# Shared expert: last group up and last two groups down as three single-pass products, with the parts formed in the tail

## The chip, the cores and the metric

The kernel runs on 1 core of one Trainium2 chip. The time is the device time of one execution in microseconds (us). The span of a profile runs from the first to the last instruction; the execution's own time is a little longer. Engines: TensorE (PE, its weight loads PEld), VectorE (DVE), ScalarE (ACT), GpSimd (POOL) and SyncE (SP), which issues most DMAs.

## The reference

Inputs: x of 64 x 32 x 512 in float32, that is 2048 tokens of 512, and a condition vector of 128 for each of the 64 blocks. In essence:

```python
h   = gelu(gelu(cond @ W0 + b0) @ W1 + b1); att = softmax(h @ W2 + b2)
xt  = einsum(att-weighted 32x32 matrices, x) + att @ bias_k    # 2048 tokens x 512
scores = softmax(xt @ router_w + router_b) + router_bias       # 16 experts, 4 groups of 4
# keep the best 2 groups, then the best 2 experts: gate, idx
y   = sum over the 2 chosen experts of gate * ((silu(xt@w1+b1) * (xt@w2+b2)) @ w3 + b3)   # inner width 128
z   = (silu(xt @ sw1 + sb1) * (xt @ sw2 + sb2)) @ sw3 + sb3    # the shared expert, inner width 256, all tokens
out = x + y + z
```

Everything is float32. This case concerns z, the shared expert.

## The kernel before, in words

The 2048 tokens are 16 tiles of 128; 4 tiles make a group (`GT` = 4, `NG` = 4 groups, 0 to 3; `EARLY` = 2, `LAST` = 3). `C` = 4 slices of 128 of the model width, `IB` = 2 blocks of 128 of the shared inner width. The order on each engine is the order written out by hand in that engine's block; engines wait for one another by counting semaphores.

**Stages.** First the mixing, the transposed activations `xT[:, g, c, :]`, the router, and the shared expert for groups 0 and 1 (upward, L891 on ACT, `shared_up` on PE; downward `shared_down`). Then a loop over tiles of tokens sorted by expert: gather by POOL, up, hidden, down on PE, scatter by POOL. Then the tail, which is what the change touches.

**Two forms of a product.** `shared_up(g, i)` (L644) sums, for w = 0, 1 and c = 0 to 3, a product of a 128x128 weight with 512 tokens. For groups 0 and 1 both operands had been split into a high part and a rest of type float32r (ACT copies the high part, L863; POOL subtracts to get the rest, L476), and the product is made of three matmuls (`PRODUCTS`: high*high, high*rest, rest*high). For groups 2 and 3 it is one float32 matmul of `sw12` and `xT`. A float32 matmul stands in the profile as two MATMUL records, a float32r one as one. `shared_down(g)` (L667) makes, for each of 4 tiles, two float32 matmuls of the hidden values `gs_of(g)` with `sw3_sb`, and one bf16 matmul with gates and biases (L687).

**The tail before the change.** PE (L806 to L815): `shared_up(2, 0)` with the last expert tile's last two steps between, `shared_up(2, 1)`, `shared_up(3, 0)`, `shared_up(3, 1)`, `shared_down(2)`, `shared_down(3)`. Blocks are numbered n = 2g + i; `shared_up` waits for `up_ready` at n - 1 (L650), which frees its PSUM bank. In `shared_down`, tile t from 8 on waits for `z_ready` at t - 3 (L679), so tile 12 waits for DVE's addition of tile 8. ACT (L968 to L977): the last expert result (L933), `shared_silu(2)`, `shared_silu(3)` (L886), then, when the rows of group 3 are loaded, four scalings (L977). POOL: the last scatter, then four additions of the scaled rows (L552), each after one scaling. DVE (L1284 to L1291): `shared_hidden(2)` (L1115, bias and multiply, two instructions), `add_rows(0)`, `add_rows(1)`, `shared_hidden(3)`, `add_rows(2)`, `shared_sum(2)`, `add_rows(3)`, `shared_sum(3)`. `add_rows(g)` (L1276) is 8 multiply-adds of expert rows into the sums (4 for group 3) and waits for the rows of its group; `shared_sum(g)` (L1196, seen as L990) adds the four PSUM tiles. SP: after the last scatter it issues 8 loads of expert rows, 2 for each group in order (L394), then stores of the 16 result tiles, each when its sum is ready (L349).

The large array `wexp` (expert weights) is free once the last expert tile is done; the rows, the hidden values of group 2 (`gs_third`) and, with the change, new parts lie in it.

Of the kernel before, what the change touches and what calls it, by code (L numbers as in the profile page):

```python
# [5 lines left out]
P = 128  # L6
ALU = mybir.AluOpType
# [12 lines left out]
def adaln_moe_ffn(nc, x, cond_pack, router_pack, shared_pack, expert_pack, expert_bias, down_bias, out):  # L20
# [40 lines left out]
    with ctx:  # L61
# [16 lines left out]

        wexp = sb("wexp", [P, E, EW])
        ebias = sb("ebias", [P, E, 2, INTER])  # L80
        shared_sb = sb("shared_sb", [P, 2 * C * SHARED + IB * DIM])
        sw12 = shared_sb[:, 0:2 * C * SHARED].rearrange("p (w c n) -> p w c n", w=2, c=C)
        sw3_sb = shared_sb[:, 2 * C * SHARED:].rearrange("p (i n) -> p i n", i=IB)

        x_early = sb("x_early", [P, EARLY * GT, DIM])
        late_region = sb("late_region", [P, 16384 // 4])
        xT = sb("xT", [P, NG, C, GN])
        r1 = sb("r1", [P, 8192 // 4])
        xt_sb = sb("xt_sb", [P, 8192 // 4])
# [35 lines left out]
        def early(rows, cols):  # L125
# [41 lines left out]
                   + [spare[:, u * DIM:(u + 1) * DIM] for u in range(2)])  # L167
        gs_third = wexp_flat[:, NG * TOPK * GT * DIM:NG * TOPK * GT * DIM + IB * GN].rearrange(
            "p (i n) -> p i n", i=IB)

# [111 lines left out]
        x_again_loaded = sem("x_again_loaded")  # L282
        rows_loaded = [sem(f"rows_loaded{g}") for g in range(NG)]
        last_scaled = sem("last_scaled")
        last_added = sem("last_added")
# [24 lines left out]
        def split_of(n):  # L310

            u = (n + EARLY * GT) % SPLITS if n < SPLITS - EARLY * GT else n - (SPLITS - EARLY * GT)
            if u < EARLY * GT:
                g, cols = u // GT, slice((u % GT) * P, (u % GT + 1) * P)
                return xT[:, g, :, cols], x_split[:, g, 0, :, cols], x_split[:, g, 1, :, cols]
            n = 2 * C * SHARED // 4
            cols = slice((u - EARLY * GT) * n, (u - EARLY * GT + 1) * n)
            return shared_sb[:, cols], w_split[:, 0, cols], w_split[:, 1, cols]

        def load_mixed(engine, g, row_groups):  # L320
# [81 lines left out]
        def _(pool):  # L402
# [143 lines left out]
            scatter(to_slot[:, :], 1)  # L546

            pool.wait_ge(x_again_loaded, 16 * (NT - EARLY * GT))
            for u in range(GT):
# [7 lines left out]
        def _(pe):  # L557
# [86 lines left out]
            def shared_up(g, i, between=()):  # L644
# [6 lines left out]
                for w in range(2):  # L651
                    for c in range(C):
                        cols = slice(i * P, (i + 1) * P)
                        if g < EARLY:
                            for n_product, (a, b) in enumerate(PRODUCTS):
                                last = mm(psum[:, bank + w, :], w12_split[:, a, w, c, cols], x_split[:, g, b, c, :],
                                          start=(c == 0 and n_product == 0),
# [9 lines left out]
            def shared_down(g, tiles=range(GT)):  # L667
                pe.wait_ge(up_ready, IB * (g + 1))
                for t in (g * GT + u for u in tiles):
# [8 lines left out]
                    elif t >= 8:  # L678
                        pe.wait_ge(z_ready, t - GT + 1)  # L679
                    bank = psum[:, DOWN_BANKS[t], :]  # L680
                    for i in range(IB):
                        mm(bank, gs_of(g)[:, i, (t % GT) * P:(t % GT + 1) * P], sw3_sb[:, i, :],
                           start=(i == 0), stop=False)

# [113 lines left out]
            with pe.If(pairs > SURE + 2):  # L798
                with pe.Fori(1, (PAIRS - SURE) // 2) as j:
                    for q in range(2):  # L800
                        p = j * 2 + SURE + q
                        with pe.If(pairs > p):
# [6 lines left out]
                                     (0, 2): lambda: down(1, last_expert, tiles, tiles_less_2)})  # L809
            shared_up(2, 1)  # L810
            shared_up(3, 0)
            shared_up(3, 1)
            pe.wait_ge(y_ready, tiles)
            shared_down(2)
            shared_down(3)  # L815


        @block.scalar
        def _(act):
# [149 lines left out]
            result(1, 1, tiles, count_of(act, N_SCATTERED + 2))  # L969
            shared_silu(2)  # L970
            shared_silu(3)

# [8 lines left out]
        def _(dve):  # L981
# [301 lines left out]

            shared_hidden(2)  # L1284
            add_rows(0)
            add_rows(1)
            shared_hidden(3)
            add_rows(2)
# [60 lines left out]
```

## Time and profile before

| what | value |
|---|---|
| median of 3 runs | 258.35 us (254.38, 258.35, 259.02) |
| the profiled execution | 256.43 us, span 254.7 us, so 1.7 us lie outside the span |
| busy share of the span | PE 92%, DVE 52%, POOL 44%, ACT 32% |
| expert loop | about 91 us to 205 us |
| tail | 205 us to 254.7 us |
| last instruction that computes | DVE's addition of tile 15, at 251.54 us |

Times in the rows are microseconds from the span's start, durations marked ns are nanoseconds. "x16" is the number of instructions; the brackets say how long the engine had been idle and what released it.

### The profile page before, as it was taken

The page shows a single profiled execution, that of the slowest core. Times are in us where ns is not written, and L with a number is a line of the kernel's source. Part 1 is how long each engine was busy: PE and PEld are TensorE (multiplying, and loading weights), DVE is VectorE, ACT ScalarE, POOL GpSimd, SP SyncE. Part 2 cuts the span into 40 slices and gives each one's busy share as a digit, 9 for nine tenths or more (in the row PEclk, how much of TensorE's full clock was granted, in tenths as well). Part 3 has the DMA queues.
Part 4 walks back from the last instruction along what each step waited for, and adds up shares of the span by engine and source line. Part 5 has one row for each costly group of instructions (what it writes and reads, how often), then busy time and mean ns, then how long its engine had stood idle before and what let it go on. Part 6 is the DMA issues. An engine that isn't in the chain of part 4 may idle for free.

```text
span 254.7 us, 3970 instructions
## 1 busy us (share of the span) xinstructions
PE 233.7 (92%) x1126; PEld 152.7 (60%) x1127; DVE 131.8 (52%) x266; ACT 81.5 (32%) x177; POOL 111.3 (44%) x136
## 2 busy tenths in 40 slices
PE   4959897999998899999999999999999699999695
PEld 4936544788744467677777777777777244444241
DVE  1294952199998873333333333333333101598982
ACT  1322787231490003333333333333333111111400
POOL 6177455900203554666656666666643310000720
PEclk9985999799999999999999999999999889999979
DMA  7999999999098389545544454555542205999753
GB/s 195 273 289 321 415 414 419 410 423 367 40 373 368 86 249 364 171 165 165 165 153 144 152 159 133 165 165 165 165 165 84 90 0 221 393 388 387 300 200 129
DMA packets 21930, 60.03 MB, mean 236 GB/s; under 512 B 2613, under 2 KB 2741, under 8 KB 21660
## 3 DMA queue, kind: packets, MB, share of 16 engines
q1 hardware_dynamic: 15164, 39.93, 42.3%
q0 software_dynamic: 5600, 17.83, 21.7%
q10 hardware_dynamic: 1152, 2.10, 2.9%
q8 instruction: 7, 0.11, 0.2%
q14 instruction: 7, 0.06, 0.1%
HBM read 43.07 MB, written 17.30 MB: 237 GB/s over the span
## 4 chain that ended last, share of the span: by engine, by line
PE 67%; DVE 20%; DMA 5%; issue 4%; ACT 2%; DVEq 0%; ACTq 0%
PE psum L559 57%; DVE late_region L990 6%; PE psum L735 6%; DMA xt_rows<-r 3%; PE psum L605 3%; DVE xT L1276 3%; DMA xT<-cond_pack 2%; DVE xT L990 2%; PE psum L748 2%; DVE r L990 1%; DVE x_early L990 1%; DVE mixed_w L1027 1%; ACT r L839 1%; DVE r L1232 0%; ACT x_split L863 0%
## 5 line engine op out<-in xcount | busy, mean ns | idle before, releaser
L559 PE MATMUL psum<-wexp,r 128*128 x272 | 68.7, 382 | 0.5 <-DVE r L1232 0.3
L559 PEld LDWEIGHTS psum<-wexp,r 128*128 128x128 f32 x272 | 48.3, 190 | 23.7 <-issue 17.7
L990 DVE TENSOR_TENSOR r<-psum,ebias 128x256 f32<-128x256 f32 x34 | 14.4, 424 | 65.2 <-PE psum L559 65.2
L508 POOL DMA_INDIRECT expert_rows<-late_region,to_row x33 | 33.4, 1011 | 33.3 <-ACT late_region L933 30.3
L498 POOL DMA_INDIRECT late_region<-xt_rows,from_row x36 | 35.3, 980 | 17.9 <-issue 8.8
L559 PE MATMUL psum<-wexp,xt_sb 128*128 x68 | 34.8, 594 | 0.0
L559 PE MATMUL psum<-xT,shared_sb 128*128 128x512 f32 x64 | 29.7, 621 | 2.5 <-issue 2.5
L927 ACT ACTIVATE r<-r 128x128 f32<-128x128 f32 x34 | 10.5, 309 | 55.6 <-DVE r L990 55.6
L933 ACT ACTIVATE late_region<-psum 128x512 f32<-128x512 f32 x34 | 20.3, 597 | 16.1 <-PE psum L559 16.1
L1232 DVE COPY r<-psum 128x512 f32<-128x512 f32 x36 | 24.5, 680 | 0.0
L559 PE MATMUL psum<-x_split,w_split 128*128 128x512 f32 x96 | 23.8, 409 | 0.3 <-DVE logits L990 0.3
L559 PEld LDWEIGHTS psum<-xT,shared_sb 128*128 128x128 f32 x64 | 12.5, 199 | 18.5 <-issue 18.5
L735 PE MATMUL psum<-ident,late_region 128*128 128x128 f32 x144 | 21.6, 273 | 0.9 <-DMA late_region<-xt_rows,from_row 0.9
L559 PEld LDWEIGHTS psum<-x_split,w_split 128*128 128x128 f32 x96 | 18.9, 199 | 4.5 <-DVE logits L990 0.4
L735 PEld LDWEIGHTS psum<-ident,late_region 128*128 128x128 f32 x144 | 17.9, 141 | 5.4 <-issue 1.9
L923 ACT ACTIVATE xt_sb<-psum 128x128 f32<-128x128 f32 x34 | 9.4, 278 | 19.7 <-PE psum L748 19.7
L552 POOL TENSOR_TENSOR xt_sb<-xt_sb,wexp 128x512 f32<-128x512 f32 x2 | 3.5, 1748 | 27.1 <-ACT wexp L977 27.1
L476 POOL TENSOR_TENSOR x_split<-xT,x_split 128x512 fp32r<-128x512 f32 x8 | 10.0, 1275 | 4.0 <-ACT x_split L863 4.0
L1041 DVE COPY xT<-psum 128x512 f32<-128x512 f32 x12 | 8.2, 687 | 6.7 <-PE psum L605 6.5
L559 PE MATMUL psum<-ident 128*128 128x128 f32 x52 | 10.0, 359 | 1.6 <-POOL ident L411 1.6
L1115 DVE SCALAR_TENSOR_TENSOR wexp<-psum,router_sb,wexp 128x512 f32<-128x512 f32 x2 | 1.5, 750 | 19.1 <-ACT wexp L886 19.1
L559 PE MATMUL psum<-shared_sb,late_region 128*128 128x512 f32 x16 | 9.1, 700 | 2.1 <-DVE xT L990 2.1
(191 smaller groups left out, 291.3 us busy)
## 6 DMA issues: line engine op xcount, KB each, us to landing
wexp<-expert_pack SPq DMA_DIRECT2D x16, 768.0 KB, 9.4
wexp<-expert_rows SPq DMA_DIRECT2D x8, 1024.0 KB, 12.9
xt_rows<-xt_sb SPq DMA_DIRECT2D x8, 256.0 KB, 8.5
xt_rows<-r SPq DMA_DIRECT2D x8, 256.0 KB, 8.8
x_early<-x SPq DMA_DIRECT2D x1, 2048.0 KB, 15.2
ebias<-expert_bias SPq DMA_DIRECT2D x1, 2048.0 KB, 11.4
out_dram<-x_early SPq DMA_DIRECT2D x8, 256.0 KB, 9.7
shared_sb<-shared_pack SPq DMA_DIRECT2D x1, 1536.0 KB, 19.6
```

The lines of the kernel that those rows point to most:

```text
L476: T.tensor_tensor(rest, whole, part, ALU.subtract).then_inc(split_ready, 1)
L498: nc.gpsimd.indirect_dma_start(out=xg[:, i % RING, :], out_offset=None, in_=xt_dram[:, :], in_offset=bass.IndirectOffsetOnAxis(ap=from_row ...
L508: nc.gpsimd.indirect_dma_start(out=y_dram[:, :], out_offset=bass.IndirectOffsetOnAxis(ap=rows.bitcast(U32), axis=0), in_=y_sb[:, slot, :], ...
L559: return nc.tensor.matmul(dst, lhsT, rhs, start=start, stop=stop)
L605: last = nc.tensor.transpose(psum[:, bank_of(t), c * P:(c + 1) * P], xt_ring[t % XR][:, c * P:(c + 1) * P], ident[:, :])
L735: last = nc.tensor.transpose(psum[:, b, c * P:(c + 1) * P], xg[:, slot, c * P:(c + 1) * P], ident[:, :])
L923: nc.scalar.activation(gT_sb[:, b, :], psum[:, 4 + b, 0:P], ACT.Copy).then_inc(gT_ready, 1)
L927: nc.scalar.activation(s_sb[:, b, :], h_sb[:, b, 0, :], ACT.Silu).then_inc(s_ready, 1)
L933: nc.scalar.activation(y_sb[:, slot, :], psum[:, 6 + b, :], ACT.Copy).then_inc(y_ready, 1)
L990: return nc.vector.tensor_tensor(dst, a, b, op)
L1041: V.tensor_copy(xT[:, t // GT, :, (t % GT) * P:(t % GT + 1) * P], psum[:, bank_of(t), :].rearrange("p (c n) -> p c n", c=C)).then_inc(xT_r ...
L1232: V.tensor_copy(xgT[:, b], psum[:, b, :].rearrange("p (c n) -> p c n", c=C)).then_inc(xgT_ready, 1)
```

## The change

Group 3's upward products and the downward products of groups 2 and 3 take the three-matmul form. Their parts are formed in the tail, beside what was there:

- ACT, after the last expert result: 8 copies for the high parts of `sw12` (4) and `xT[:, 3]` (4), then SiLU of block (2, 0), 2 copies for `sw3`, the copy of hidden block (2, 0), SiLU (2, 1), copy (2, 1), and then for each block of group 3 its SiLU and its copy, the copy waiting for DVE's hidden value.
- DVE: 8 subtractions for the rests of `sw12` and `xT[:, 3]`; `shared_hidden(2, [1])` is now behind `add_rows(0)`; after `shared_hidden(LAST)` come 2 subtractions for the rests of group 3's hidden values.
- POOL: 2 subtractions for `sw3` and 2 for the hidden values of group 2, between the last scatter and the additions of rows.
- PE: a wait for the 8 parts ahead of `shared_up(3, 0)`, waits for the parts ahead of each `shared_down`.
- Rests are written over the wholes or into `r1`; high parts go to the free end of `wexp`. No DMA is added.

```diff
...
@@ -165,8 +171,22 @@
                    + [spare[:, u * DIM:(u + 1) * DIM] for u in range(2)])
-        gs_third = wexp_flat[:, NG * TOPK * GT * DIM:NG * TOPK * GT * DIM + IB * GN].rearrange(
-            "p (i n) -> p i n", i=IB)
+        gs_at = NG * TOPK * GT * DIM
+        gs_third = wexp_flat[:, gs_at:gs_at + IB * GN].rearrange("p (i n) -> p i n", i=IB)
+        free_part = wexp_part[:, :, :].rearrange("p e n -> p (e n)")[:, gs_at + IB * GN:]
+        n12, n3, ngs = 2 * C * SHARED, IB * DIM, IB * GN
+        w12_last = [a.rearrange("p (w c n) -> p w c n", w=2, c=C) for a in (free_part[:, 0:n12], r1_part[:, :])]
+        w3_late = [a.rearrange("p (i n) -> p i n", i=IB)
+                   for a in (free_part[:, n12:n12 + n3], shared_part[:, n12:])]
+        x_last = [free_part[:, n12 + n3:n12 + n3 + C * GN].rearrange("p (c n) -> p c n", c=C),
+                  xT_part[:, NG - 1, :, :]]
+        gs_parts = {g: [a.rearrange("p (i n) -> p i n", i=IB) for a in (free_part[:, at:at + ngs], low)]
+                    for g, at, low in (
+                        (2, n12 + n3 + C * GN,
+                         wexp_part[:, :, :].rearrange("p e n -> p (e n)")[:, gs_at:gs_at + ngs]),
+                        (3, n12 + n3 + C * GN + ngs, late_part[:, 0:ngs]))}
         ident = sb("ident", [P, P])
...
@@ -316,6 +343,16 @@
             return shared_sb[:, cols], w_split[:, 0, cols], w_split[:, 1, cols]
+        LAST_SPLITS = 2 * C
+        def last_split_of(n):
+            c = n % C
+            if n < C:
+                w, c0 = n // 2, 2 * (n % 2)
+                return [a[:, w, c0:c0 + 2, :] for a in (sw12, *w12_last)]
+            return [a[:, c, :] for a in (xT[:, NG - 1], *x_last)]
         def load_mixed(engine, g, row_groups):
...
@@ -545,6 +582,15 @@
             scatter(to_slot[:, :], 1)
+            for i in range(IB):
+                pool.wait_ge(w3_hi_ready, i + 1)
+                T.tensor_tensor(w3_late[1][:, i], sw3_sb[:, i], w3_late[0][:, i], ALU.subtract
+                                ).then_inc(w3_lo_ready, 1)
+            for i in range(IB):
+                pool.wait_ge(gs_hi_ready, i + 1)
+                T.tensor_tensor(gs_parts[2][1][:, i], gs_of(2)[:, i], gs_parts[2][0][:, i], ALU.subtract
+                                ).then_inc(gs_lo_ready, 1)
             pool.wait_ge(x_again_loaded, 16 * (NT - EARLY * GT))
...
@@ -651,9 +697,11 @@
                         cols = slice(i * P, (i + 1) * P)
-                        if g < EARLY:
+                        if g != 2:
                             for n_product, (a, b) in enumerate(PRODUCTS):
-                                last = mm(psum[:, bank + w, :], w12_split[:, a, w, c, cols], x_split[:, g, b, c, :],
+                                weights = w12_split[:, a, w, c, cols] if g < EARLY else w12_last[a][:, w, c, cols]
+                                x_cols = x_split[:, g, b, c, :] if g < EARLY else x_last[b][:, c, :]
+                                last = mm(psum[:, bank + w, :], weights, x_cols,
                                           start=(c == 0 and n_product == 0),
...
@@ -678,9 +726,14 @@
                     bank = psum[:, DOWN_BANKS[t], :]
+                    cols = slice((t % GT) * P, (t % GT + 1) * P)
                     for i in range(IB):
-                        mm(bank, gs_of(g)[:, i, (t % GT) * P:(t % GT + 1) * P], sw3_sb[:, i, :],
-                           start=(i == 0), stop=False)
+                        if g < EARLY:
+                            mm(bank, gs_of(g)[:, i, cols], sw3_sb[:, i, :], start=(i == 0), stop=False)
+                        else:
+                            for n_product, (a, b) in enumerate(PRODUCTS):
+                                mm(bank, gs_parts[g][b][:, i, cols], w3_late[a][:, i, :],
+                                   start=(i == 0 and n_product == 0), stop=False)
                     if t == 0:
...
@@ -808,10 +861,14 @@
             shared_up(2, 1)
+            pe.wait_ge(last_lo_ready, LAST_SPLITS)
             shared_up(3, 0)
             pe.wait_ge(y_ready, tiles)
+            pe.wait_ge(w3_lo_ready, IB)
+            pe.wait_ge(gs_lo_ready, IB)
             shared_down(2)
+            pe.wait_ge(gs_last_lo_ready, IB)
             shared_down(3)
...
@@ -967,8 +1024,23 @@
             result(1, 1, tiles, count_of(act, N_SCATTERED + 2))
-            shared_silu(2)
-            shared_silu(3)
+            for m in range(LAST_SPLITS):
+                whole, hi, _ = last_split_of(m)
+                nc.scalar.activation(hi, whole, ACT.Copy).then_inc(last_hi_ready, 1)
+            def hidden_hi(g, i):
+                act.wait_ge(up_ready, g * IB + i + 1)
+                nc.scalar.activation(gs_parts[g][0][:, i], gs_of(g)[:, i], ACT.Copy).then_inc(gs_hi_ready, 1)
+            shared_silu(2, [0])
+            for i in range(IB):
+                nc.scalar.activation(w3_late[0][:, i], sw3_sb[:, i], ACT.Copy).then_inc(w3_hi_ready, 1)
+            hidden_hi(2, 0)
+            shared_silu(2, [1])
+            hidden_hi(2, 1)
+            for i in range(IB):
+                shared_silu(3, [i])
+                hidden_hi(3, i)
             act.wait_ge(rows_loaded[LAST], 16 * TOPK)
...
@@ -1281,10 +1353,23 @@
                         link(ins)
-            shared_hidden(2)
+            for m in range(LAST_SPLITS):
+                dve.wait_ge(last_hi_ready, m + 1)
+                whole, hi, lo = last_split_of(m)
+                tt(lo, whole, hi, ALU.subtract).then_inc(last_lo_ready, 1)
+            def hidden_lo(i):
+                dve.wait_ge(gs_hi_ready, IB + i + 1)
+                tt(gs_parts[LAST][1][:, i], gs_of(LAST)[:, i], gs_parts[LAST][0][:, i], ALU.subtract
+                   ).then_inc(gs_last_lo_ready, 1)
+            shared_hidden(2, [0])
             add_rows(0)
+            shared_hidden(2, [1])
             add_rows(1)
-            shared_hidden(3)
+            shared_hidden(LAST)
+            for i in range(IB):
+                hidden_lo(i)
             add_rows(2)
...
```

## Rows read from the trace of the kernel before

**Rows 1.** The page: busy shares; the chain that ended last, by engine.

```profile
PE 233.7 (92%) x1126; PEld 152.7 (60%) x1127; DVE 131.8 (52%) x266; ACT 81.5 (32%) x177; POOL 111.3 (44%) x136
...
PE 67%; DVE 20%; DMA 5%; issue 4%; ACT 2%; DVEq 0%; ACTq 0%
```

**Rows 2.** Chain of waits, 205 to 255 us: start, us, what.

```profile
205.12 26.90 PE psum L559 x62
...
241.00 0.70 DVE xT L990
...
241.84 9.69 PE psum L559 x20
...
251.54 0.69 DVE xT L990
```

**Rows 3.** Timeline of DVE: start, us, line, tiles [idle before].

```profile
219.76 11.08 DVE L1276 SCALAR_TENSOR_TENSOR x_early<-wexp,tops,x_early 128x512 f32<-128x512 f32 x16
...
233.43 7.54 DVE L1276 SCALAR_TENSOR_TENSOR xT<-wexp,tops,xT 128x512 f32<-128x512 f32 x8
241.00 2.48 DVE L990 TENSOR_TENSOR xT<-xT,psum 128x512 f32<-128x512 f32 x4
```

**Rows 4.** Timeline of ACT from 204 us.

```profile
207.15 0.60 ACT L933 ACTIVATE late_region<-psum 128x512 f32<-128x512 f32 x1 [1.72 <-PE psum L559]
211.44 0.69 ACT L886 ACTIVATE wexp<-psum,router_sb 128x512 f32<-128x512 f32 x1 [3.70 <-PE psum L559]
218.31 0.69 ACT L886 ACTIVATE wexp<-psum,router_sb 128x512 f32<-128x512 f32 x1 [6.18 <-PE psum L559]
...
232.04 0.69 ACT L886 ACTIVATE late_region<-psum,router_sb 128x512 f32<-128x512 f32 x1 [6.18 <-PE psum L559]
```

**Rows 5.** Timeline of PEld, 45 to 70 us: weight loads of block (1, 0), three products.

```profile
63.48 5.33 PEld L559 LDWEIGHTS psum<-x_split,w_split 128*128 128x128 f32 x24
```

**Rows 6.** Timeline of PE, two tiles of the downward product of group 2.

```profile
231.84 1.88 PE L559 MATMUL psum<-shared_sb,wexp 128*128 128x512 f32 x4
...
233.78 1.88 PE L559 MATMUL psum<-shared_sb,wexp 128*128 128x512 f32 x4
```

**Rows 7.** Timeline of ACT, 44 to 71 us: four copies of high parts.

```profile
43.90 2.18 ACT L863 ACTIVATE x_split<-xT 128x512 fp32r<-128x512 f32 x4
```

**Rows 8.** Instructions of lines 863 and 476: ns min/median/max, first and last start.

```profile
L863 ACT ACTIVATE x_split<-xT x8: 617/626/657, 34.7 to 45.5; 128x512 fp32r<-128x512 f32 x8
...
L476 POOL TENSOR_TENSOR x_split<-xT,x_split x8: 1271/1274/1278, 35.6 to 48.3; 128x512 fp32r<-128x512 f32 x8
```

**Rows 9.** Line 394 alone at 212.2 us: the second load of rows.

```profile
L394 SPq DMA_DIRECT2D wexp<-expert_rows x1: 495/495/495, 212.2 to 212.2; - x1
DMA to landing us min/median/max: 7.5/7.5/7.5
```

**Rows 10.** Timeline of ACT: the scalings, released by the last load.

```profile
236.10 2.56 ACT L977 ACTIVATE wexp<-wexp,tops 128x512 f32<-128x512 f32 x4 [3.37 <-DMA wexp<-expert_rows]
```

**Rows 11.** Timelines of DVE and POOL, 236 to 242 us, where both run.

```profile
236.19 1.42 DVE L1276 SCALAR_TENSOR_TENSOR xT<-wexp,tops,xT 128x512 f32<-128x512 f32 x2
237.52 1.77 DVE L1276 SCALAR_TENSOR_TENSOR xT<-wexp,tops,xT 128x512 f32<-128x512 f32 x1
239.22 1.75 DVE L1276 SCALAR_TENSOR_TENSOR xT<-wexp,tops,xT 128x512 f32<-128x512 f32 x1
236.97 3.45 POOL L552 TENSOR_TENSOR xt_sb<-xt_sb,wexp 128x512 f32<-128x512 f32 x2 [27.08 <-ACT wexp L977]
240.38 2.95 POOL L552 TENSOR_TENSOR xT<-xT,wexp 128x512 f32<-128x512 f32 x2
```

**Rows 12.** Busy time by stretch, PE alone: stretch, busy (count), PEclk.

```profile
240.00:241.00 1.00, 0.00 (x0) 1.00 0.29 111
...
243.00:244.00 1.00, 1.00 (x2) 0.54 1.01 375
...
246.00:247.00 1.00, 1.00 (x3) 0.75 0.00 0
```

More of the change, by code:

```diff
@@ L76, in adaln_moe_ffn, with sb_and_parts @@
         HALF = E // 2
-        wexp = sb("wexp", [P, E, EW])
+        def sb_and_parts(name, shape):
+            with nc.sbuf_tensor(name + "_part", shape, F32R) as part:
+                pass
+            return sb(name, shape), part
+        wexp, wexp_part = sb_and_parts("wexp", [P, E, EW])
         ebias = sb("ebias", [P, E, 2, INTER])
-        shared_sb = sb("shared_sb", [P, 2 * C * SHARED + IB * DIM])
+        shared_sb, shared_part = sb_and_parts("shared_sb", [P, 2 * C * SHARED + IB * DIM])
         sw12 = shared_sb[:, 0:2 * C * SHARED].rearrange("p (w c n) -> p w c n", w=2, c=C)
@@ L85, in adaln_moe_ffn @@
         x_early = sb("x_early", [P, EARLY * GT, DIM])
-        late_region = sb("late_region", [P, 16384 // 4])
-        xT = sb("xT", [P, NG, C, GN])
-        r1 = sb("r1", [P, 8192 // 4])
+        late_region, late_part = sb_and_parts("late_region", [P, 16384 // 4])
+        xT, xT_part = sb_and_parts("xT", [P, NG, C, GN])
+        r1, r1_part = sb_and_parts("r1", [P, 8192 // 4])
         xt_sb = sb("xt_sb", [P, 8192 // 4])
@@ L283, in adaln_moe_ffn @@
         rows_loaded = [sem(f"rows_loaded{g}") for g in range(NG)]
+        last_hi_ready = sem("last_hi_ready")
+        last_lo_ready = sem("last_lo_ready")
+        w3_hi_ready = sem("w3_hi_ready")
+        w3_lo_ready = sem("w3_lo_ready")
+        gs_hi_ready = sem("gs_hi_ready")
+        gs_lo_ready = sem("gs_lo_ready")
+        gs_last_lo_ready = sem("gs_last_lo_ready")
         last_scaled = sem("last_scaled")
```

## The prediction

> **What bounds the kernel now.** I read the page first, then the chain of waits of the tail, then each engine's timeline over the same stretch. PE is busy 92% of the span, and the chain of work is PE's for 67% of it [rows 1]. That share is an average over stages, though. The change touches only what comes after 205 us, so the chain there is what counts [rows 2]. It is PE's own for 26.9 us, to 232.0 us. Then it leaves PE: it runs through DVE's additions of expert rows to 241.0 us. PE has group 2 down done at 239.6 us (four tiles from 231.84 us, each 1.94 us after the one before [rows 6]) and then waits for DVE's first sum at 241.0 us. The last four tiles are PE's again, 241.84 to 251.52 us, and DVE's last addition starts at 251.54 us.
>
> So a faster PE before 241 us is worth nothing by itself; what DVE does from 219.76 us on sets when the last four tiles may begin. DVE's list is full there: 16 multiply-adds in 11.08 us (0.693 us each), group 3's hidden values, and `add_rows(2)` in 7.54 us from 233.43 us [rows 3]. It is this list that the change makes longer and ties to ACT.
>
> **The change part by part.** All times are on the profiled execution, 256.43 us with a span of 254.7 us; the median of the runs is 258.35 us, 1.9 us more.
>
> *PE, shorter products.* A float32 block of `shared_up` takes 6.87 us (the SiLUs that end them stand at 211.44 and 218.31 us) [rows 4]. The same block in three passes: 24 weight loads in 5.33 us, so (5.33 - 0.19) / 23 = 0.2235 us each and 5.36 us a block [rows 5]. Saved: 1.5 us a block, 3.0 us for two. A downward tile goes from 1.94 us (231.84 to 233.78) [rows 6] to 6 + 1 instructions of 0.2235 = 1.56 us; saved 0.38 us a tile, 1.5 us a group. In all 6.0 us of PE work go.
>
> *Parts of the weights and of xT.* ACT ends the last expert result at 207.75 us [rows 4]. Eight copies at 0.545 us (four took 2.18) [rows 7] end at 212.1 us. DVE's eight subtractions: no row has this subtraction on DVE; the first can begin 0.63 us [rows 8] after 207.75 us. Below stands 0.62 us each (four additions with one operand in PSUM in 2.48 us), above 1.75 us (two SBUF operands while POOL also runs) [rows 3, 11]; POOL is nearly idle there, so I take 0.65 us, 208.4 to 213.6 us; by the upper end it is 222.4 us. PE needs them at 218.3 us, so they cost nothing in the forecast; the cover is `shared_up(2)`, and by the upper end PE would wait 4 us. SiLU (2, 0) moves from 211.44 to 212.1 us and its hidden value to 213.6 us, also covered. ACT's two copies of `sw3` end at 213.9 us; POOL's subtractions at 1.27 us [rows 8] end near 217.3 us with the first hidden block, against a need at 231 us: nothing.
>
> *`shared_hidden(2, [1])` behind `add_rows(0)`.* This is the first new wait. `add_rows(0)` waits for the rows of group 0, that is the second load: 212.2 + 7.5 = 219.7 us [rows 9]. Its 8 instructions (5.54 us) end at 225.2 us, the hidden value of (2, 1) at 225.95 us instead of 219.8 us. Block (3, 1) is n = 7 and waits for `up_ready` at 6, which is this value. PE, after 218.3 + 5.36 = 223.6 us, stands still until 226.0 us: 2.4 us, most of the 3.0 us just saved. Behind the same value on ACT stand its copy (2, 1) and then SiLU (3, 0), so these move to 226 to 227.2 us.
>
> *POOL against `add_rows(1)`.* POOL's subtraction for (2, 1) runs at about 226.6 us, while DVE is in `add_rows(1)`. What such a meeting costs is in [rows 11]: a multiply-add takes 1.75 to 1.77 us beside POOL against 0.7 us alone (two in 1.42 us), so 1.0 us. `add_rows(1)`: 225.95 + 5.54 + 1.0 = 232.5 us (bounds 0 and 1.0).
>
> *The ladder for group 3.* This is the second new wait, and the dearer one. Before, both SiLUs of group 3 were done or ready when DVE came, and DVE went on at 233.43 us. Now ACT may not do SiLU (3, 1) before its copy of block (3, 0), and that copy waits for DVE. In order: DVE hidden (3, 0) 232.5 to 233.2; ACT copy 0.63, to 233.8, then SiLU (3, 1), 0.69, to 234.5 [rows 4, 8]; DVE hidden (3, 1) to 235.3; ACT copy to 235.9; DVE's two subtractions, one behind hidden (3, 1) and one behind the copy, to 236.6. PE's block (3, 1) is done by 226.0 + 5.36 = 231.4 us, before its SiLU is asked for, so PE's gain buys nothing here. `add_rows(2)` starts at 236.6 us instead of 233.43 us: 3.1 us late.
>
> *`add_rows(2)` against POOL.* The last load lands at 236.0 us and frees the scalings at 236.10 us [rows 10]; ACT is free at 235.9 us. So POOL's four additions start at 237.0 us as before. Before, half of `add_rows(2)` was over by then and two of its instructions were slowed, by 1.0 us each [rows 11]. Now all of it lies beside POOL. Bounds: two slowed as before, or four, one for each of POOL's additions. I take three, since in [rows 11] the second of the pair from 236.19 us kept its length (it ended at 237.61 us) although POOL had begun at 236.97 us. That is 5.54 + 3.0 = 8.6 us, ending at 245.2 us (244.2 to 246.2), 4.2 us later than before.
>
> The Trainium skill, GPSIMD Engine Reference, in its table of specifications, says that POOL's SBUF interfaces are shared with VectorE and contend with DVE instructions in a 2-port mode or with two SBUF inputs. Taken to the letter every overlapped multiply-add pays, which makes it four and 1.0 us more at the end; the first instruction in the rows did not pay.
>
> *The last four tiles.* The first sum frees tile 12 at 245.2 + 0.84 = 246.0 us (before, 241.00 to 241.84). PE has had nothing since 231.4 + 4 x 1.56 = 237.6 us, 8.4 us. Before, it paused 2.2 us, and the granted clock was then about 0.5 from 243 us to the middle of the microsecond that shows 0.75, so some 3.4 us [rows 12], 1.2 GHz instead of 2.4, a loss of about 1.7 us. Four tiles warm are 6.2 us. With one such stretch: 6.2 + 1.7 + 0.2 = 8.1 us, PE done at 254.1 us; with two, 255.8 us. Before it took 9.68 us. So of group 3's 1.5 us all stays, and DVE's chain has eaten it first. I take one stretch and half of another's risk: last addition at 254.8 us against 251.54 us. The last store behind it is unchanged.
>
> **Sum.** +3.1 (ladder, first wait and POOL) + 1.0 (POOL in `add_rows(2)`) + 0.1 - 1.6 (last tiles) + 0.7 (clock) = +3.3 us. On the profiled execution 259.7 us; on the median 261.6 us. The runs before spread over 4.6 us, and the profiled one lies 1.9 us under the median; I put 260.5 us, between the two.
>
> **The rivals.**
> *A, PE's gain comes through (faster side, within 2%).* If DVE's waits turned out free (`add_rows(2)` at 233.4 us, ending 241.0 us), only the last tiles would shrink: 241.84 + 8.1 = 249.9 us, 1.6 us less: 254.8 us profiled, 256.7 us on the median. For it: 6.0 us of PE work really go, and PE holds 67% of the chain. Against it: `shared_hidden(2, [1])` stands in the code behind a load that lands at 219.7 us.
> *B, the clock (slower by over 2%).* The place is the last four tiles and block (3, 1). If PE stays at the low level for all 28 products of the last four tiles, they take 28 x 0.447 = 12.5 us instead of 8.1, so the last addition starts at 258.5 us: +7.0 us, 263.4 us profiled, 265.4 us on the median. It decides from +5.2 us, that is from 1.9 us more loss than I count, 3.8 us more at the low level. For it: PE now pauses twice, 2.4 us and 8.4 us, where 2.2 us were followed by half the clock. Against: after that pause it was back within 5 us of work.
> *C, a wash.* The three overlaps with POOL do not bite and the ladder is cheaper than its steps (copies 0.55 us): the delay of 4.2 us shrinks to 1.6 us, which the tiles give back; 258.4 us on the median. That is also what would be seen if the three-pass blocks did not run in 5.36 us but as slowly as before and DVE alone decided.
>
> **How the numbers follow.** Forecast 0.60, A 0.13, B 0.15, C 0.12. The range 256.5 to 264.5 us holds A's time, C, and the forecast with its bounds (two or four slowed instructions, one or two slow stretches: -1.7 to +2.7 us); B's far part is left out. A difference of 2%, 5.2 us, is about what a measurement of this kernel can tell from no change. Faster by over 2% would need more than the 1.6 us that any chain here offers: 0.03. Slower by over 2%: B and the upper end of the forecast, 0.18. Within 2%: 0.79.
>
> **What would show it.** In the changed profile: 24 weight loads of a block of group 3 in about 5.3 us; PE idle about 2.4 us before block (3, 1), released by DVE's hidden value near 226 us; DVE idle in front of the second hidden value of group 3, released by ACT; `add_rows(2)` starting near 236.6 us with three multiply-adds above 1.5 us; PE idle some 8 us before tile 12 and a granted clock near 0.5 after it. I am wrong if `add_rows(2)` starts before 235 us, or if PE goes from (3, 0) to (3, 1) without a pause, or if the subtractions on DVE take over 1 us each.

## The result: 1.9% slower, and where it went

The changed kernel takes 259.83 us in the median (257.5 to 262.4, 4 runs) against 256.47 us (254.38 to 259.02, 4 runs) of the kernel before: ratio 1.0192, 95% interval 1.0128 to 1.0257. The ratio compares only the faster executions of each kernel, so it is not the quotient of the two medians, which is 1.013. Run again beside other kernels later it gave 1.0191 (1.0119 to 1.0264). The profiled execution took 258.33 us with a span of 256.5 us.

The profiles differ by only 1.9 us. Their stages ahead of the tail, which the change does not touch, differ too: the last expert result ends at 207.75 us before and at 206.03 us after. More of the early work ran at half clock in the profile of before; that this is all of the 1.7 us is not shown. Busy time of each engine in one early stretch, with PEclk (the granted clock of PE as a share of 2.4 GHz) third from the end, before and after:

```profile
40.00:50.00 10.00, 8.16 (x42) 5.93 (x42) 1.41 (x5) 4.58 (x9) 7.75 (x7) 0.83 1.04 417
```

```profile
40.00:50.00 10.00, 8.17 (x46) 6.04 (x46) 1.52 (x5) 4.29 (x8) 8.00 (x7) 1.00 1.03 416
```

I measure everything from the end of the last expert result: the **tail**, to the end of DVE's last addition, is 44.48 us before (252.23 - 207.75) and 47.99 us after (254.02 - 206.03). That is +3.5 us, 1.4% of the time; the ratio's interval begins at 1.3%. In a second profile of the changed kernel (below) the tail is 49.33 us, +4.85 us or 1.9%.

The page after (busy; the chain by engine), for [rows 1]:

```profile
PE 226.1 (88%) x1158; PEld 157.1 (61%) x1159; DVE 140.8 (55%) x276; ACT 89.0 (35%) x191; POOL 116.6 (45%) x140
...
PE 53%; DVE 24%; DMA 13%; issue 5%; ACT 3%; SPq 0%; DVEq 0%; POOL 0%; POOLq 0%; ACTq 0%
```

PE has lost 7.6 us of busy time and the kernel is slower: PE's share of the chain fell from 67% to 53%, DVE's and DMA's grew. The chain of waits of the tail (start, us, what), for [rows 2]:

```profile
210.48 7.55 DMA wexp<-expert_rows
218.03 0.03 issue
218.06 2.75 DVE x_early L1348 x4
...
223.57 0.66 DVE wexp L1187
...
230.67 0.67 DVE late_region L1187
231.34 0.02 issue
231.37 0.63 ACT wexp_part L1033
232.00 0.59 ACT late_region L943
232.58 0.03 issue
232.61 0.76 DVE late_region L1187
233.37 0.02 issue
233.39 0.64 ACT wexp_part L1033
...
244.97 8.34 PE psum L605 x28
253.31 0.02 issue
253.33 0.69 DVE xT L1062
```

Before, PE stood in this chain until 232.0 us. Now, from 210.48 us on, the chain is the load of group 0's rows and then DVE, and between 230.67 and 233.39 us it climbs the ladder: DVE hidden block, ACT copy, ACT SiLU, DVE hidden block, ACT copy. DVE's timeline, for [rows 3]:

```profile
224.15 6.52 DVE L1348 SCALAR_TENSOR_TENSOR x_early<-wexp,tops,x_early 128x512 f32<-128x512 f32 x8
230.59 0.74 DVE L1187 SCALAR_TENSOR_TENSOR late_region<-psum,router_sb,late_region 128x512 f32<-128x512 f32 x1
232.61 0.75 DVE L1187 SCALAR_TENSOR_TENSOR late_region<-psum,router_sb,late_region 128x512 f32<-128x512 f32 x1 [1.28 <-ACT late_region L943]
233.28 1.47 DVE L1062 TENSOR_TENSOR late_region_part<-late_region,wexp_part 128x512 fp32r<-128x512 f32 x2
234.67 9.43 DVE L1348 SCALAR_TENSOR_TENSOR xT<-wexp,tops,xT 128x512 f32<-128x512 f32 x8
```

POOL's four additions stand beside the last of these lines:

```profile
235.44 3.46 POOL L598 TENSOR_TENSOR xt_sb<-xt_sb,wexp 128x512 f32<-128x512 f32 x2 [8.75 <-ACT wexp L1049]
238.86 3.37 POOL L598 TENSOR_TENSOR xT<-xT,wexp 128x512 f32<-128x512 f32 x2
```

`add_rows(2)` starts 28.64 us into the tail instead of 25.68, and takes 9.4 us instead of 7.5. PE's waits from 220 us on (engine, line, what for: us in total, times, longest), and its granted clock (stretch, busy, PEclk), for [rows 12]:

```profile
PE psum L605 <- DVE xT L1062: 6.9, 1, 6.9
PE psum L605 <- DVE wexp L1187: 2.3, 1, 2.3
```

```profile
224.00:228.00 4.00, 3.71 (x9) 0.57 1.05 387
241.00:245.00 4.00, 0.03 (x1) 0.58 0.00 0
245.00:246.00 1.00, 1.00 (x3) 0.50 0.41 127
...
248.00:249.00 1.00, 1.00 (x5) 0.77 0.34 123
```

Both pauses are there and in this profile both are followed by work at 1.2 GHz. The account: +2.96 (later start of `add_rows(2)`), +1.90 (its length, to the first sum), -1.35 (from the first sum to the end, 11.23 to 9.88 us) = +3.5 us.

### The profile page after: what moved, and what is told of

It is laid out like the page before. It is cut to its first block, busy times and chain, and to the rows that moved or that the text cites. A ratio compares the mean times of both kernels' runs of the same rounds, so it can differ in the third digit from the quotient of the medians.

```text
span 256.5 us, 4064 instructions
## 1 busy us (share of the span) xinstructions
PE 226.1 (88%) x1158; PEld 157.1 (61%) x1159; DVE 140.8 (55%) x276; ACT 89.0 (35%) x191; POOL 116.6 (45%) x140
## 4 chain that ended last, share of the span: by engine, by line
PE 53%; DVE 24%; DMA 13%; issue 5%; ACT 3%; SPq 0%; DVEq 0%; POOL 0%; POOLq 0%; ACTq 0%
PE psum L605 45%; DVE late_region L1062 6%; PE psum L788 6%; DVE x_early L1348 4%; DMA xt_rows<-xt_sb 4%; DMA xt_rows<-r 3%; DVE xT L1348 3%; DMA wexp<-expert_rows 3%; DMA xT<-cond_pack 2%; PE psum L801 2%; PE psum L651 1%; DVE r L1062 1%; DMA expert_rows<-late_region,to_slot 1%; DVE xT L1062 1%; DVE x_early L1062 1%
## 5 line engine op out<-in xcount | busy, mean ns | idle before, releaser
L605 PE MATMUL psum<-wexp_part 128*128 128x512 f32 x40 | 17.5, 470 | 9.2 <-DVE xT L1062 6.9
L605 PE MATMUL psum<-x_split,w_split 128*128 128x512 f32 x96 | 22.4, 392 | 0.6 <-DVE logits L1062 0.3
L605 PEld LDWEIGHTS psum<-x_split,w_split 128*128 128x128 f32 x96 | 17.9, 188 | 4.6 <-DVE xt_sb L1187 0.5
L605 PE MATMUL psum<-xT,shared_sb 128*128 128x512 f32 x32 | 14.2, 595 | 2.8 <-issue 2.8
L605 PEld LDWEIGHTS psum<-wexp_part 128*128 128x128 f32 x40 | 8.4, 211 | 11.6 <-issue 7.4
L1348 DVE SCALAR_TENSOR_TENSOR x_early<-wexp,tops,x_early 128x512 f32<-128x512 f32 x16 | 12.0, 810 | 6.0 <-DMA wexp<-expert_rows 5.9
L605 PEld LDWEIGHTS psum<-xT,shared_sb 128*128 128x128 f32 x32 | 5.9, 190 | 10.6 <-issue 10.6
L1348 DVE SCALAR_TENSOR_TENSOR xT<-wexp,tops,xT 128x512 f32<-128x512 f32 x10 | 10.8, 1136 | 0.0
```

The lines of the kernel that those rows point to most:

```text
L605: return nc.tensor.matmul(dst, lhsT, rhs, start=start, stop=stop)
L1348: ins = V.scalar_tensor_tensor(out=acc_tile(t), in0=rows_k[:, g, k, t % GT, :], scalar=tops[:, k, t:t + 1], in1=acc_tile(t), op0=ALU.mult, ...
```

## Experiments

All tails are from the end of the last expert result to the end of DVE's last addition. "Start" is that of `add_rows(2)`, "length" from there to the first sum of group 2, "rest" what follows. Each row's times are those of one profiled execution. Each ratio is against the kernel before on the same chip. The intervals are 0.7 to 2% wide, so what 1 or 2 us between two kernels come from is read from the traces, not from the ratios.

| kernel | start | length | rest | tail | ratio (95%) |
|---|---|---|---|---|---|
| before | 25.68 | 7.57 | 11.23 | 44.48 | 1 |
| changed | 28.64 | 9.47 | 9.88 | 47.99 | 1.019 (1.013-1.026) |
| changed, again | 28.85 | 9.47 | 11.01 | 49.33 | 1.019 (1.012-1.026) |
| e1_order | 28.33 | 9.45 | 9.64 | 47.42 | 1.024 (1.018-1.030) |
| e2_order_silu | 26.87 | 9.45 | 10.40 | 46.72 | 1.011 (1.003-1.019) |
| e3_down3_f32 | 27.12 | 9.50 | 12.30 | 48.92 | 1.022 (1.012-1.032) |
| e10_down3_order | 25.47 | 7.55 | 12.38 | 45.40 | 1.012 (1.006-1.018) |
| e4_warm | 28.54 | 9.47 | 8.23 | 46.24 | 1.019 (1.009-1.029) |
| e9_before_warm | 25.68 | 7.57 | 9.54 | 42.79 | 0.999 (0.992-1.005) |
| e6_after_no_pool | 28.58 | 5.54 | 10.41 | 44.53 | 1.007 (1.003-1.012) |
| e7_before_no_pool | 25.68 | 5.54 | 10.41 | 41.63 | 0.989 (0.982-0.996) |
| e5_up_only | 24.96 | 5.54 | 9.63 | 40.13 | 0.982 (0.976-0.988) |
| e8_up_no_pool | 24.50 | 5.54 | 10.41 | 40.45 | 0.984 (0.980-0.987) |

**The changed kernel again** (no edit).

> The changed kernel once more, unedited, beside the two kernels of this call. Tail 47.5 to 48.5 us; add_rows(2) starts 28.3 to 28.9 us after the last expert result and takes 9.4 to 9.5 us; time 1.3 to 2.5% above the kernel before. If instead the tail is near 46 us, the first profile of it was not typical and the account of 3.5 us falls.

Start and length repeat to 0.2 us. The tail is 0.8 us above the expected band, all in the last tiles, 9.46 us instead of 8.34. PEclk of this run:

```profile
244.00:246.00 2.00, 1.58 (x4) 0.50 0.42 156
...
248.00:250.00 2.00, 2.00 (x6) 0.50 0.07 26
250.00:252.00 2.00, 2.00 (x10) 0.91 0.36 134
```

Half clock lasted 6.0 us into the last tiles here, past 250 us, against 3.5 us in the first profile. The length of such a stretch after a long pause varies from run to run; the delay of DVE does not.

PE's first pause went the other way. It was 2.5 us long, and block (3, 1) behind it ran at full clock, 5.7 us from 223.72 us on, where it took 7.4 us at first. PE's wait, and then its PEclk:

```profile
PE psum L605 <- DVE wexp L1187: 2.5, 1, 2.5
```

```profile
223.00:229.00 6.00, 5.28 (x23) 1.00 1.05 387
```

The start of `add_rows(2)` moved by only 0.2 us, so the half clock of that block did no harm in this kernel.

**Order, step one** (e1_order).

```diff
-            shared_hidden(2, [0])
+            shared_hidden(2)
             add_rows(0)
-            shared_hidden(2, [1])
             add_rows(1)
```

> The changed kernel with group 2's second hidden block ahead of add_rows(0) again, as it was before the change. Measure: the tail, from the end of the last expert result on ACT to the end of DVE's last addition, 44.5 us before the change (207.75 to 252.23) and 48.0 us after it (206.03 to 254.02). Theory (DVE's list and its ladder with ACT decide): PE's pause of 2.3 us ahead of block (3, 1) goes, so PE is done with that block 2 to 4 us sooner, but the ladder still begins when add_rows(1) ends, so add_rows(2) starts at most 0.7 us sooner and the tail stays at 47.3 to 48.0 us. Rival (PE's pause is what costs): the tail falls by 2.3 us or more, to 45.7 us or below.

47.42 us, as the theory said. PE's first pause is gone, and its block (3, 1) ends early for nothing: ACT's copy of block (3, 0) waits 8.3 us for DVE.

```profile
234.05 0.74 DVE L1187 SCALAR_TENSOR_TENSOR late_region<-psum,router_sb,late_region 128x512 f32<-128x512 f32 x1
236.07 0.75 DVE L1187 SCALAR_TENSOR_TENSOR late_region<-psum,router_sb,late_region 128x512 f32<-128x512 f32 x1 [1.27 <-ACT late_region L943]
...
234.83 0.63 ACT L1033 ACTIVATE wexp_part<-late_region 128x512 fp32r<-128x512 f32 x1 [8.30 <-DVE late_region L1187]
```

**Order, step two** (e2_order_silu), e1's edit and:

```diff
+            shared_silu(3)
             for i in range(IB):
-                shared_silu(3, [i])
                 hidden_hi(3, i)
```

> As the kernel with group 2's second hidden block ahead of add_rows(0), and on ACT both SiLUs of group 3 ahead of both copies; the work is the same as after the change. Theory: the rungs of the ladder go. DVE does both hidden blocks back to back (1.4 us), one copy stays in the open (0.63 us), then two subtractions (1.3 us). Against the order SiLU, copy, SiLU, copy that saves DVE's wait of 1.28 us and a part of the copy, so add_rows(2) starts about 1.0 to 1.3 us sooner; with POOL's four additions at the same time as before, one of them meets less, so the tail is 46.0 to 47.2 us. Rival (the work of the subtractions, not the order, costs; or the end is set by PE): 47.5 us or more.

46.72 us, within the band. The start falls by 1.5 us against e1, though not one copy or subtraction was removed: that is the price of the rungs. The length did not fall; even at 26.87 us all four of the second half's multiply-adds are still ahead when POOL begins.

**Group 3's downward product in float32** (e3_down3_f32; the rest of `sw3` also goes to its own place, so that the whole stays).

```diff
-                        if g < EARLY:
+                        if g != 2:
                             mm(bank, gs_of(g)[:, i, cols], sw3_sb[:, i, :], start=(i == 0), stop=False)
...
-                shared_silu(3, [i])
-                hidden_hi(3, i)
+            shared_silu(3)
...
-            for i in range(IB):
-                hidden_lo(i)
```

> The changed kernel with group 3's downward product as float32 again: no copies and no subtractions of its hidden blocks, everything else as after the change. Theory: add_rows(2) starts after add_rows(1) and two hidden blocks, 2.6 us sooner than in the changed kernel, so that fewer of its multiply-adds meet POOL (two or three instead of four, 1 to 2 us); the last four tiles take 1.5 us more at full clock, 9.7 us or so. Tail 44.5 to 46.0 us. Rival (PE's last tiles decide): the tail grows by 1.5 us, to 49.5 us.

A miss: the tail stayed at 48.92 us. The start fell by only 1.5 us instead of 2.6, and no meeting with POOL was saved. The chain of waits says what took the ladder's place:

```profile
227.62 0.67 DVE wexp L1185
...
228.34 7.35 PE psum L606 x24
...
235.72 0.70 ACT late_region L943
```

DVE's late hidden value (2, 1) lets PE's block (3, 1) begin, and that block, 3.4 us of it at half clock after the pause, takes 7.35 us. Its PEclk (stretch, busy, PEclk):

```profile
228.00:230.00 2.00, 1.66 (x5) 0.78 1.05 387
230.00:232.00 2.00, 2.00 (x6) 0.50 1.04 384
232.00:234.00 2.00, 2.00 (x9) 0.87 1.05 387
```

So PE's first pause, harmless behind the ladder, was the next bound, together with the half clock after it. That was not in my theory, and the next run takes both away. The two are not told apart: by an estimate, with the block at the 5.7 us of the changed kernel's second profile, PE would be done at 234.1 us, DVE would have gone on without its wait of 1.04 us, and `add_rows(2)` would have started near 26.0 us, as expected. (This profile is of an execution of 263.2 us, and e3's median is 259.7; the medians, 259.7 for e3 and 256.8 for the next kernel, point the same way.)

**The same with DVE's order of before** (e10_down3_order), e3's edits and e1's.

> The changed kernel with group 3's downward product as float32 and, in addition, group 2's second hidden block ahead of add_rows(0) again. The kernel with the first edit alone had a tail of 48.9 us, with PE pausing 2.4 us ahead of block (3, 1), that block then taking 7.35 us at half clock in part, and ACT waiting for it. Theory (in that kernel PE's pause had taken the ladder's place; the two only pay when both go): no pause, block (3, 1) done near 21.5 us from the last expert result, add_rows(2) starts at 25.5 to 26.0 us instead of 27.1, two of its multiply-adds meet POOL instead of four, so it takes 7.6 us; last tiles 9.7 us (a pause of 6 us ahead of them, half clock); tail 44.3 to 45.0 us. Rival (the pause was harmless, the remaining copies and subtractions cost): 48 us or more.

The start falls to 25.47 us and the length to 7.55 us: two meetings with POOL instead of four. The tail, 45.40 us, is 0.4 us above the band, because the last tiles took 10.84 us, the half clock lasting longer than before (6.8 us). Taking away the first wait alone gave 0.3 us of the start (e1), the ladder alone 1.5 us in a profile with the half clock (e3), both together 3.2 us. Yet without both waits the kernel is still 1.2% slower than the one before.

**PE kept busy ahead of tile 12** (e4_warm; the products' result is not used).

```diff
             pe.wait_ge(gs_last_lo_ready, IB)
+            for _ in range(7):
+                mm(psum[:, 0, :], ident[:, :], x_early[:, 0, :])
             shared_down(3)
```

> The changed kernel with seven float32 products of 512 columns into a free PSUM bank, 6.0 us of PE work, in PE's pause of about 7 us ahead of tile 12; their result is not used. Theory: the granted clock stays at 1.0 over the last tiles, which then take 6.4 to 6.6 us instead of 8.3, so the tail is 46.2 us (46.0 to 46.8): DVE's sums of tiles 12 to 15 follow each other with little idle time. Rival (the clock falls for another reason than the pause, or DVE is the bound of the last tiles anyway): tail 47.5 to 48.0 us.

46.24 us, and the chain has the last tiles at 6.69 us instead of 8.34:

```profile
244.15 6.69 PE psum L605 x28
...
250.86 0.69 DVE xT L1064
```

**The same in the kernel before** (e9_before_warm), with two products instead of seven.

> The kernel before the change with two float32 products of 512 columns (1.7 us of PE work, result not used, into a free PSUM bank) in PE's pause of 2.1 us ahead of tile 12. Theory (the pause brings the half clock, and the half clock costs 1.9 us of the 9.7 us of the last tiles): the granted clock stays at 1.0, the last tiles take 7.8 to 8.0 us, tail from the end of the last expert result 42.5 to 43.0 us instead of 44.5. Rival (the clock falls whatever PE does there, or DVE is the bound): 44.0 to 44.6 us.

42.79 us; the last tiles take 8.00 us instead of 9.69, and PEclk is 1.00 where it was 0.54 [rows 12]:

```profile
243.00:245.00 2.00, 1.82 (x5) 1.00 0.56 207
```

So where the last tiles ran at half clock in the kernel before, it cost 1.7 us. That the long pause brings it is borne out by e4: each of the seven profiled pauses of 3 us and more in the tails of these runs was followed by half clock, and with the pause filled up to its last 2.5 us the clock stayed up. For the short pause of the kernel before, one profile of e9 is weak evidence: e5 below has a pause of 2.2 us at the same place, unfilled, and keeps its clock. The timed ratios of both runs (0.999, and 1.019 as for the changed kernel) do not show a gain: 1.7 us is 0.7%, and the intervals are 1.3 and 2% wide.

**POOL's four additions done by DVE** (e6_after_no_pool on the changed kernel, e7_before_no_pool on the one before). ACT's scalings and POOL's additions of group 3 are taken out, and:

```diff
-                ks = range(TOPK) if g < LAST else [0]
+                ks = range(TOPK)
...
-                        if g == LAST:
-                            dve.wait_ge(last_added, t % GT + 1)
```

> The changed kernel with ACT's four scalings and POOL's four additions for group 3 taken out and done by DVE as four more multiply-adds in add_rows(3) (2.8 us). Theory (two-input instructions of POOL and DVE take turns, 1.0 us a meeting, and in the changed kernel there are four such meetings in add_rows(2)): add_rows(2) falls from 9.5 to 5.6 us, the first sum of group 2 comes 3.9 us sooner, add_rows(3) becomes 5.5 us and lies beside PE's last tiles. Tail 44.0 to 44.8 us instead of 48.0. Rival (DVE's four more instructions cost as much as the meetings): tail 47 us or more.

> The kernel before the change with the same move of group 3's additions from ACT and POOL to DVE. Theory: add_rows(2) falls from 7.6 to 5.6 us, so tile 12 may begin 2.0 us sooner, when PE has only just finished group 2: its pause goes, and with it the half clock (1.9 us). PE's tiles end at about 39.9 us from the last expert result, DVE's add_rows(3) at 39.3 us, tail 40.8 to 41.5 us instead of 44.5. Rival (2.8 us more on DVE in front of the last sums outweigh 2.0 us): tail 44.5 to 45.5 us.

44.53 us and 41.63 us: 3.5 and 2.9 us less, the second 0.1 us above its band. `add_rows(2)` is 5.51 and 5.50 us in both, so the 1.9 us by which its length differed between the two kernels was POOL. (ACT's scalings were taken out as well, but in the changed kernel they end at 237.1 us, and slowed multiply-adds follow until 242.8 us.) DVE's timeline of e6 and of e7:

```profile
235.78 5.51 DVE L1333 SCALAR_TENSOR_TENSOR xT<-wexp,tops,xT 128x512 f32<-128x512 f32 x8
```

```profile
232.78 5.50 DVE L1261 SCALAR_TENSOR_TENSOR xT<-wexp,tops,xT 128x512 f32<-128x512 f32 x8
```

**Only group 3's upward products in three passes** (e5_up_only): both downward products float32, no parts for them, DVE's order as before. **The same with POOL's additions on DVE** (e8_up_no_pool).

```diff
-            shared_hidden(2, [0])
+            shared_hidden(2)
             add_rows(0)
-            shared_hidden(2, [1])
             add_rows(1)
             shared_hidden(LAST)
-            for i in range(IB):
-                hidden_lo(i)
...
-                        if g < EARLY:
+                        if True:
                             mm(bank, gs_of(g)[:, i, cols], sw3_sb[:, i, :], start=(i == 0), stop=False)
```

> Only group 3's upward products in three passes, with their 8 copies and 8 subtractions; both downward products float32 as before the change, DVE's order as before. Times from the end of the last expert result. Theory (PE's shorter blocks are worth something when DVE gets no new waits): PE has block (3, 1) done near 21 us instead of 24.3 us, DVE goes from add_rows(1) through both hidden blocks without a wait and starts add_rows(2) at 24.9 us (25.7 before the change, 28.6 after it); POOL's additions start at 29.3 us as always and meet one or two of its multiply-adds; tail 41.3 to 43.2 us, so 1.3 to 3.2 us below the kernel before. Rival (the upward product's new parts already cost what PE gains): tail 44.5 us or more.

> Group 3's upward products in three passes as in the up-only kernel, and group 3's additions on DVE. Theory (DVE is then the bound of the end: 8 multiply-adds, 4 sums, 8 multiply-adds, 4 sums after 24.9 us): tail 41.0 to 41.8 us, no better than the kernel before with the same move, because PE's earlier end buys nothing. Rival (PE's gain of 3 us adds to the move): tail 38 to 39 us.

e5 beats both kernels: 251.29 us in the median against 255.91 us of the kernel before in the same session, ratio 0.982 (0.976 to 0.988). Its tail is 1.2 us below the expected band. DVE:

```profile
230.96 1.41 DVE L1169 SCALAR_TENSOR_TENSOR late_region<-psum,router_sb,late_region 128x512 f32<-128x512 f32 x2
232.28 5.50 DVE L1330 SCALAR_TENSOR_TENSOR xT<-wexp,tops,xT 128x512 f32<-128x512 f32 x8
237.82 2.48 DVE L1044 TENSOR_TENSOR xT<-xT,psum 128x512 f32<-128x512 f32 x4
240.22 3.38 DVE L1330 SCALAR_TENSOR_TENSOR xt_sb<-wexp,tops,xt_sb 128x512 f32<-128x512 f32 x2
```

Both hidden blocks stand back to back (1.41 us for two), and `add_rows(2)` is over just after POOL begins (237.16 us): its last instruction was already running and kept its length. Two meetings come later, in `add_rows(3)` (3.38 us for two). The chain is DVE's alone from 225.53 us to the end, but PE's last product ends only at 246.64 us, so by an estimate without these meetings the end would come 0.1 us sooner. PE pauses ahead of tile 12 as in the kernel before, and this time the clock stays up (wait; PEclk):

```profile
PE psum L597 <- DVE xT L1044: 2.2, 1, 2.2
```

```profile
236.00:240.00 4.00, 1.84 (x5) 1.00 1.05 405
```

So of the 4.35 us by which the tail is shorter than before, 0.7 us is the earlier start (DVE no longer waits 1.3 us for the SiLU behind PE's block (3, 1)), 2.0 us is two meetings with POOL missed, and 1.6 us is the rest, in which the kernel before had 3.4 us at half clock. How often the clock stays up there is not known from one profile; the four timed runs lie within 1.0 us (250.98 to 252.02).

e8, where DVE is the bound, ends at 40.45 us, 0.6 us below its band, and adds nothing to e5. It is 1.2 us better than e7, the same move in the kernel before, all of it in the start (24.50 against 25.68 us), so PE's shorter blocks were worth something there too, against the expectation. The ratio of e8 is not told apart from e5's.

e10 against e5 gives the price of group 2's downward product alone in three passes, parts included, since they differ in nothing else: 5.3 us of tail. The start is 0.5 us later, because POOL's subtraction for a hidden block meets `add_rows(0)` (e10's chain has four multiply-adds in 3.78 us, where four undisturbed ones take 2.75); that is enough for `add_rows(2)` to meet POOL twice, 2.0 us; and PE, which is done sooner, pauses 6.0 us ahead of tile 12 instead of 2.2, with half clock after it, 2.75 us.

```profile
219.55 3.78 DVE x_early L1346 x4
```

## Why the prediction was right, point by point

The sign and the mechanism of the delay held: DVE's list ties to ACT, starts `add_rows(2)` late and meets POOL more often. The time put down, 260.5 us, lies close to the measured median, 259.83 us, but part of that is luck. The median of the kernel before was 256.47 us in the comparison and not 258.35, so +3.3 us on it is 259.8 us; the timed ratio of 1.9% is nearer to 4.9 us. In the tail +3.3 us was forecast and +3.5 and +4.85 us were measured in two profiles, and in the first of them two errors offset each other: POOL in `add_rows(2)` cost 0.9 us more than its term, the last part 0.55 us less (-1.35 against -0.8). The upper bound of "-1.7 to +2.7 us" is also too wide: one more slowed instruction and a second slow stretch give +2.0 us.

- *Shorter products.* Block (3, 0) took 24 products at 0.227 us (the second at 216.62, the 24th at 221.61 us); forecast 0.2235.
- *Parts.* DVE's eight subtractions took 0.62 to 0.63 us each (2.52 and 2.48 us for four), the lower bound, and were hidden.
- *First wait.* PE paused 2.29 us, forecast 2.4. I did not count that block (3, 1) could then run at half clock: it went from 224.29 to about 231.7 us, 7.4 us instead of 5.36, ending just before ACT could take it. In the second profile it ran at full clock, and the start was the same; in e3 it was the bound.
- *POOL in `add_rows(1)`.* 6.52 us instead of 5.54: +1.0, as forecast.
- *Ladder.* Start +2.96 us against +3.1. e2 shows that half of it is order and not work (1.5 us). By its letter one sign of being wrong came true: `add_rows(2)` starts at 234.67 us, before 235 us. But this profile's tail begins 1.72 us sooner than the one the forecast was worked out on; on that one's clock the start is at 236.39 us, against 236.6.
- *POOL in `add_rows(2)`.* Forecast three slowed instructions, 8.6 us; measured 9.43, that is 3.9 us above the 5.5 of e6, four meetings. This term was undersized by 0.9 us (+1.9 against +1.0). The rule of the Trainium skill (GPSIMD Engine Reference, table of specifications) that a DVE instruction with two SBUF inputs contends with POOL gave four. The trace agrees in that four were slowed, one for each addition of POOL; a fifth, already running when POOL's first addition began, kept its 0.75 us, as the one in [rows 11] did.
- *Last tiles.* Forecast 8.1 us with one slow stretch, up to 9.8 with two; measured 8.34 and, in the second profile, 9.46. The pause ahead of them, forecast 8.4 us, was 6.9 us where block (3, 1) had run partly at half clock and 8.5 us where it had not.
- *Rival A* (PE's gain comes through) was wrong for this change. In e5 a part of it does gain, but not as A says: there the last tiles keep their float32 products. *Rival B* (the clock stays low) did not occur: in the second profile the last tiles took 1.4 us more than the 8.1 us forecast, against the 4.4 us of B. *Rival C* needed cheap meetings and rungs; both had their full price.

One statement of the working was wrong: that a faster PE before 241 us is worth nothing by itself, and that no chain here offers more than 1.6 us. Before the change DVE waited 1.3 us for the SiLU that PE's block (3, 1) released:

```profile
232.76 0.75 DVE L1115 SCALAR_TENSOR_TENSOR late_region<-psum,router_sb,late_region 128x512 f32<-128x512 f32 x1 [1.26 <-ACT late_region L886]
```

A start 0.7 us sooner also took `add_rows(2)` out of POOL's way. So what I left out altogether is that the upward and the downward halves of the change have opposite signs. The upward half alone is worth -4.4 us of tail in its profile (1.6 us of it in the part where the clock matters), the downward half, with the order of instructions that came with it, costs the 7.9 us between e5 and the changed kernel; 5.3 us of these stay when the new waits are gone and only group 2's downward product is in three passes (e10).

## What to carry to other kernels

Before an engine's work is made shorter, look who holds its consumer: here PE's 3 us in the upward products were worth having by themselves, and were lost when the downward products were shortened too, whose parts DVE, ACT and POOL had to make in front of the rows. Put what other engines wait for ahead of instructions that wait for a DMA, and do all of one kind (both SiLUs) before what waits for the reply. Work given to POOL to relieve DVE is free only while DVE runs nothing with two SBUF inputs: 4 additions cost DVE 2.0 us in one place and 3.9 us three microseconds later, where doing them on DVE costs 2.8. A small delay can cost more than itself when it moves an instruction into another engine's way: 0.5 us of start brought 2.0 us of meetings (e10 against e5).

## What the runs showed of the hardware

A multiply-add of DVE with two SBUF inputs beside a POOL addition takes 1.63 to 1.78 us instead of 0.75, once for each POOL addition that it meets; one that was already running when POOL's first addition began kept its 0.75 us (before, changed, e5). The POOL addition takes 1.71 us instead of 1.27. A DVE sum with one operand in PSUM keeps its 0.69 us beside POOL.

Short pauses of PE in the tail came with either clock afterwards. Work at 1.2 GHz followed pauses of 2.1 us (before), 2.2 (e6), 2.3 (changed) and 2.4 us (e3); work at 2.4 GHz followed pauses of 2.1 and 2.5 us (e4), 2.2 (e5) and 2.5 us (changed, second profile). All seven pauses from 3.0 to 10.7 us were followed by work at 1.2 GHz. After pauses of 6.9 and 8.5 us the slow stretch ended 3.5 us into the last tiles in one run and 6.0 us in another, of the same kernel.
